# Sums of the first GNN step during the count matrix build, and GCN sums of two groups in turns

## What is computed

```python
h = jnp.maximum(_layernorm(x), 0.0)
# _L0_gnn_ref
h = jnp.tanh(h @ W_in + b_in)
for _ in range(12):
    agg = segment_sum(h[src], dst) / deg
    diff = jnp.tanh(gelu(agg @ W1 + b1) @ W2 + b2)
    h = h + (diff - decay * h) * 0.5
x = x + h
# _L1_gnn_ref, with loops added to the edges
h = jnp.maximum(_layernorm(x), 0.0)
h = relu(gcn_conv(h, W1, b1))        # gcn_conv: sum over edges of (h @ W)[src] * norm
x = x + gcn_conv(h, W2, b2)
```

## Time and profile before

| | us |
|---|---|
| median of 3 runs | 1339.37 |
| lowest, highest | 1339.19, 1340.59 |
| the profiled execution | 1339.52 |
| its span, first to last instruction | 1337.8 |
| TensorE busy in it | 1267.6 (95%) |
| VectorE busy | 400.9 (30%) |
| ScalarE busy | 314.6 (24%) |
| batches of the build | about 36 to 136 |
| twelve GNN steps | about 137 to 1181 |
| first GCN layer, second | about 1181, 1260 to the end |

### The profile page before, as it was taken

One profiled execution on the slowest core, in us unless ns is written; L12 is line 12 of the kernel. 1 busy time (PEld: TensorE's weight loads), 2 busy tenths in 40 slices (PEclk: granted clock), 3 DMA queues, 4 the chain that ended last, 5 costly groups with the idle time before them and its releaser, 6 DMA issues.

```text
span 1337.8 us, 17376 instructions
## 1 busy us (share of the span) xinstructions
PE 1267.6 (95%) x7201; PEld 712.3 (53%) x7201; DVE 400.9 (30%) x817; ACT 314.6 (24%) x449; POOL 43.5 (3%) x48
## 2 busy tenths in 40 slices
PE   2875899999999999999999999999999999979998
PEld 1764356456565564655645556456564564545545
DVE  7899113113121130121311312113122132472312
ACT  1788213113121131221311312113122131120100
POOL 4800000000000000000000000000000000000000
PEclk7899999999999999999999999999999999999999
DMA  3000200000000000000000000000000001120101
GB/s 97 1 1 0 62 0 1 0 0 0 0 0 0 0 0 0 0 0 0 0 0 0 0 0 0 0 0 0 0 0 0 0 0 40 48 59 0 49 17 33
DMA packets 24541, 13.66 MB, mean 10 GB/s; under 512 B 6171, under 2 KB 23605, under 8 KB 24384
## 3 DMA queue, kind: packets, MB, share of 16 engines
q1 hardware_dynamic: 22414, 12.28, 3.5%
q10 hardware_dynamic: 1698, 0.66, 0.2%
q0 software_dynamic: 400, 0.33, 0.1%
HBM read 9.42 MB, written 3.44 MB: 10 GB/s over the span
## 4 chain that ended last, share of the span: by engine, by line
PE 88%; DVE 7%; issue 2%; DMA 2%; ACT 0%; DVEq 0%; SPq 0%; POOL 0%; ACTq 0%; POOLq 0%
PE ps L623 66%; PE ps L670 10%; PE ps L661 9%; DVE scratch L1014 4%; PE ps L560 1%; PE ps L708 1%; DVE lo L997 1%; DMA adj<-packed_scratch,adj 1%; DMA dinv_scratch<-cols 0%; PE ps L552 0%; DMA adj<-adj 0%; PE ps L523 0%; PE ps L549 0%; DVE cols L1189 0%; DMA adj<-in_dst_dram 0%
## 5 line engine op out<-in xcount | busy, mean ns | idle before, releaser
L623 PE MATMUL ps<-adj,hi 128*128 128x512 f16 (+2 forms) x2450 | 805.8, 352 | 14.1 <-DVE lo L997 9.4
L623 PE MATMUL ps<-adj,lo 128*128 128x512 f16 (+2 forms) x2352 | 787.3, 352 | 0.0
L623 PEld LDWEIGHTS ps<-adj,hi 128*128 128x128 f16 x2450 | 237.9, 97 | 260.5 <-issue 18.8
L623 PEld LDWEIGHTS ps<-adj,lo 128*128 128x128 f16 x2352 | 228.8, 97 | 241.7 <-issue 20.6
L1120 DVE TENSOR_TENSOR ps<-ps,bias 128x512 f32<-128x512 f32 (+1 forms) x84 | 53.9, 642 | 546.5 <-PE ps L670 546.5
L825 ACT ACTIVATE scratch<-ps 128x512 f32<-128x512 f32 (+1 forms) x84 | 46.3, 551 | 630.2 <-DVE ps L1120 630.0
L670 PEld LDWEIGHTS ps<-w,scratch 128*128 128x128 f32 x1200 | 144.2, 192 | 8.1
L670 PE MATMUL ps<-w,scratch 128*128 128x128 f32 x1200 | 146.1, 275 | 0.0
L816 ACT ACTIVATE scratch<-ps,b1c,cols 128x512 f32<-128x512 f32 (+2 forms) x168 | 112.0, 723 | 144.8 <-PE ps L661 143.9
L661 PE MATMUL ps<-scratch,w 128*128 128x512 f32 (+2 forms) x336 | 137.8, 538 | 0.0
L1113 DVE TENSOR_TENSOR scratch<-ps,scratch 128x512 f32<-128x512 f32 (+2 forms) x84 | 52.0, 620 | 179.7 <-PE ps L661 132.1
(11 more groups left out here) (129 smaller groups left out, 207.2 us busy)
## 6 DMA issues: line engine op xcount, KB each, us to landing
scratch<-rdeg_scratch SPq DMA_DIRECT2D x1, 1562.5 KB
state<-in_x_dram SPq DMA_DIRECT2D x5, 256.0 KB, 4.6
scratch<-in_x_dram SPq DMA_DIRECT2D x5, 256.0 KB, 2.8
x_scratch<-state SPq DMA_DIRECT2D x5, 256.0 KB, 2.7
scratch<-dinv_scratch SPq DMA_DIRECT2D x5, 256.0 KB, 3.8
state<-x_scratch SPq DMA_DIRECT2D x5, 256.0 KB, 4.3
out_dram<-state SPq DMA_DIRECT2D x5, 256.0 KB
adj<-adj SPq DMA_DIRECT2D x1, 390.6 KB, 4.0
```

The lines of the kernel that those rows point to most:

```text
L623: return nc.tensor.matmul(bank, values[:, k, :], adj[:, k, c0:c0 + n], start=is_first, stop=is_last)
```

## The change

Three things are changed.

*Early sums.* The last 18 batches are no loop any more. Behind each batch TensorE sums two source tiles (`EARLY_TILES`) of the first step: 24 tiles of group 0 into bank 7, then 12 tiles of group 1 into bank 6, in the order `K_FIRST`, which puts the short tile last. The last window moves to bank 0. If the edge list needs the general path (`missed`, not taken with this input), they are summed again.

*The first step.* It is written out (`first_step`) on TensorE, ScalarE and VectorE. Five banks are used for the seven sums (`FIRST_BANK`); each group's tiles but the short one come first, then a wait for `s_pair`, then the short tile. `outputs` and `hidden` come one group later. Behind the last sum: `outputs(3)`, `hidden(4)`, 4 tiles of step 1, `outputs(4)`, `hidden(5)`, `hidden(6)`, 4 more tiles, `outputs(5)`, `outputs(6)`. The loop does 10 steps.

*The first GCN layer.* Behind the 4 tiles of group 0: tiles 4 to 11 of group 0, 0 to 11 of group 1, 12 to 19 of group 0, 12 to 19 of group 1 (places in `K_ORDER`), then the rest of each. VectorE makes `norm_lo(2)` earlier.

The core of the diff. Left out are helpers (`hidden`, `outputs`, `gelu`, `tanh`, `means` and others) that move out of `step` and get `t` as an argument, with `means` reading the bank of `FIRST_BANK` in the first step.

```diff
@@ -46,6 +46,8 @@
 SPANS = [(k0 * P, min(nt * P, NODES - k0 * P)) for k0, nt in GROUPS]
 K_ORDER = [(k, g) for g, (k0, nt) in enumerate(GROUPS[:TAIL]) for k in range(k0, k0 + nt) if k != SHORT]
 K_ORDER += [(SHORT, TAIL - 1), (GROUPS[TAIL][0], TAIL)]
+K_FIRST = [e for e in K_ORDER if e[0] != SHORT] + [e for e in K_ORDER if e[0] == SHORT]
+FIRST_BANK = [7, 6, 0, 1, 2, 6, 7]
 HEAD = 2 * GROUP_TILES
 LAST_HEAD = GROUP_TILES
 
@@ -66,6 +68,9 @@
 PROD_AT = [b + EVERY // 2 for b in TURN_AT]
 LO_AT = [b + 4 for b in PROD_AT]
 ENTRY_BATCHES = (LO_AT[-1] + 2) // 2 * 2
+EARLY_TILES = 2
+EARLY = EARLY_TILES * (BATCHES - ENTRY_BATCHES)
+EARLY_PARTS = [(0, min(EARLY, FULL)), (0, max(EARLY - FULL, 0))]
 PACK = 4096
 LANES = 32
 BLOCK = NODES // 5
@@ -576,11 +581,24 @@
                     entry_transpose(TURN_AT.index(b))
                 if b in PROD_AT:
                     entry_product(PROD_AT.index(b))
-            with pe.Fori(ENTRY_BATCHES // 2, BATCHES // 2) as i:
-                for u in range(2):
-                    multiply(u, i)
+            def first_sums(g, part):
+                c0, n = SPANS[g]
+                for at in range(*part):
+                    k = K_FIRST[at][0]
+                    for values in (hi, lo):
+                        if values is hi or k != SHORT:
+                            mm = nc.tensor.matmul(ps[:, FIRST_BANK[g], 0:n], values[:, k, :], adj[:, k, c0:c0 + n],
+                                                  start=(at == 0 and values is hi), stop=(k == SHORT))
+                return mm
+
+            pe.wait_ge(s_lo, NG)
+            for b in range(ENTRY_BATCHES, BATCHES):
+                multiply(b % 2, b // 2)
+                for place in range((b - ENTRY_BATCHES) * EARLY_TILES, (b - ENTRY_BATCHES + 1) * EARLY_TILES):
+                    first_sums(place // FULL, (place % FULL, place % FULL + 1))
             pe.wait_ge(s_last[0], 1)
-            window(0, 0, ps[:, 6, :], 0).then_inc(s_last[1], 1)
+            pe.wait_ge(s_ev[0], BATCHES // 2 + OPEN)
+            window(0, 0, ps[:, 0, :], 0).then_inc(s_last[1], 1)
 
             missed = pe.value_load(flag[0:1, 0:1], min_val=0, max_val=1)
 
...
                     pe.wait_ge(s_diag, 1)
                     edge_sums(STEPS, 0, (c_hi[0], c_lo[0]), 0, (0, LAST_HEAD))
                 else:
                     edge_sums(t + 1, 0, (s_hi, s_lo), (t + 1) * NG, (0, HEAD))
-                outputs(TAIL - 1)
-                outputs(TAIL)
-
-            edge_sums(0, 0, (s_hi, s_lo), 0, (0, HEAD))
-            with pe.Fori(0, STEPS - 1) as t:
+                outputs(t, TAIL - 1)
+                outputs(t, TAIL)
+
+            def first_step():
+                for g in range(NG):
+                    at = EARLY_PARTS[g][1] if g < 2 else 0
+                    if at < FULL:
+                        first_sums(g, (at, FULL))
+                    pe.wait_ge(s_pair, 16)
+                    c0, n = SPANS[g]
+                    bank = ps[:, FIRST_BANK[g], 0:n]
+                    with pe.If(missed != 0):
+                        with pe.Fori(0, TILES) as r:
+                            add_rest(0, g, bank, r)
+                    first_sums(g, (FULL, TILES)).then_inc(s_agg, 1)
+                    if g >= 3:
+                        outputs(0, g - 3)
+                    if g >= 2:
+                        hidden(0, g - 2)
+                edge_sums(1, 0, (s_hi, s_lo), NG, (0, GROUP_TILES))
+                outputs(0, TAIL - 2)
+                hidden(0, TAIL - 1)
+                hidden(0, TAIL)
+                edge_sums(1, 0, (s_hi, s_lo), NG, (GROUP_TILES, HEAD))
+                outputs(0, TAIL - 1)
+                outputs(0, TAIL)
+
+            first_step()
+            with pe.Fori(1, STEPS - 1) as t:
                 step(t, False)
             step(STEPS - 1, True)
 
@@ -710,13 +758,17 @@
                                               start=True, stop=True)
                     mm.then_inc(c_out[layer], 1)
 
+                if layer == 0:
+                    pe.wait_ge(s_diag, 2)
+                    for part in ((0, LAST_HEAD, 12), (1, 0, 12), (0, 12, 20), (1, 12, 20)):
+                        edge_sums(STEPS, part[0], (c_hi[0], c_lo[0]), 0, part[1:])
                 for g in range(NG):
                     if 2 <= g < TAIL:
                         pe.wait_ge(c_aggT[layer], g - 1)
                     if layer == 0:
                         pe.wait_ge(s_diag, g + 1)
                     edge_sums(STEPS + layer, g, (c_hi[layer], c_lo[layer]), 0,
-                              (LAST_HEAD if layer == 0 and g == 0 else 0, TILES)).then_inc(c_agg[layer], 1)
+                              (20 if layer == 0 and g < 2 else 0, TILES)).then_inc(c_agg[layer], 1)
                     if g >= 1:
                         product(g - 1)
                     if layer == 0 and g == 3:
...
-            with act.Fori(0, STEPS - 1) as t:
+                        next_hi(t, g)
+
+            act.wait_ge(s_now, 1)
+            gelu(0, 0)
+            for g in range(3):
+                tanh(0, g)
+                gelu(0, g + 1)
+            act.wait_ge(s_agg, NG)
+            next_hi(0, 0)
+            next_hi(0, 1)
+            tanh(0, 3)
+            gelu(0, 4)
+            next_hi(0, 2)
+            next_hi(0, 3)
+            tanh(0, 4)
+            gelu(0, 5)
+            gelu(0, 6)
+            next_hi(0, 4)
+            tanh(0, 5)
+            tanh(0, 6)
+            next_hi(0, 5)
+            next_hi(0, 6)
...
-                means(TAIL)
+                means(t, TAIL)
                 norm_lo(0)
-                add_bias(TAIL - 2)
+                add_bias(t, TAIL - 2)
                 norm_lo(1)
-                update(TAIL - 2)
+                update(t, TAIL - 2)
+                norm_lo(2)
                 add_input(TAIL - 2)
                 row_factors(12, 20)
                 norm_rows(3)
-                add_bias(TAIL - 1)
-                norm_lo(2)
+                add_bias(t, TAIL - 1)
                 norm_rows(4)
-                update(TAIL - 1)
+                update(t, TAIL - 1)
                 norm_lo(3)
                 add_input(TAIL - 1)
                 norm_lo(4)
-                add_bias(TAIL)
-                update(TAIL)
+                add_bias(t, TAIL)
+                update(t, TAIL)
...
-            with dve.Fori(0, STEPS - 1) as t:
+            def first_step():
+                step_scales(0)
+                means(0, 0, True)
+                means(0, 1, True)
+                for g in range(3):
+                    add_bias(0, g)
+                    update(0, g)
+                    means(0, g + 2, True)
+                dve.wait_ge(s_now, 1)
+                next_lo(0, 0)
+                add_bias(0, 3)
+                next_lo(0, 1)
+                update(0, 3)
+                means(0, 5, True)
+                means(0, 6, True)
+                add_bias(0, 4)
+                next_lo(0, 2)
+                update(0, 4)
+                next_lo(0, 3)
+                next_lo(0, 4)
+                add_bias(0, 5)
+                update(0, 5)
+                add_bias(0, 6)
+                update(0, 6)
+                next_lo(0, 5)
+                dve.wait_ge(s_hi, 2 * NG)
+                V.tensor_copy(now_keep, keep)
+                next_lo(0, 6)
+
+            first_step()
+            with dve.Fori(1, STEPS - 1) as t:
                 step(t, False)
             step(STEPS - 1, True)
```

More of the change, by code:

```diff
@@ L614, in _, with add_rest @@
                 pe.wait_ge(g_degk, 5 + OPEN)
+                for g in range(2):
+                    first_sums(g, EARLY_PARTS[g])
+            def add_rest(turn, g, bank, r):
+                n = SPANS[g][1]
+                pe.wait_ge(s_rest[g], (turn * TILES + r + 1) * 16)
+                nc.tensor.matmul(bank, hi[:, bass.ds(r, 1), :].rearrange("p k f -> p (k f)"), rest_tile[:, 0:n],
+                                 start=False, stop=False)
+                nc.tensor.matmul(bank, lo[:, bass.ds(r, 1), :].rearrange("p k f -> p (k f)"), rest_tile[:, 0:n],
+                                 start=False, stop=False).then_inc(s_restu, 1)
             def edge_sums(turn, g, split, first, part=(0, TILES)):
@@ L642, in edge_sums @@
                             with pe.Fori(0, TILES) as r:
[L643 to L647, removed]
+                                add_rest(turn, g, bank, r)
                     product(hi, k, at == 0, False)
@@ L654, in _, with hidden, outputs @@
             pe.wait_ge(s_w, 16 * 8)
-            def step(t, last):
[L656 to L673, removed]
+            def hidden(t, g):
+                n = SPANS[g][1]
+                pe.wait_ge(s_aggT, t * NG + g + 1 + OPEN)
+                pe.wait_ge(s_gelu, t * 2 * NG + (2 * g if g < TAIL else 0) + OPEN)
+                for h in range(2):
+                    nc.tensor.matmul(ps_hid_tail[h] if g == TAIL else ps_hid[h][:, 0:n], w1[:, h * FEAT:(h + 1) * FEAT],
```

(26 more changed lines are left out.)

136 lines of the change are left out of this document (69 added, 67 removed).

## The result

The changed kernel takes 1324.93 us (median of 4, 1324.38 to 1325.52) where the kernel before, run beside it, takes 1339.98: ratio 0.9889, 95% interval 0.9877 to 0.9901. The forecast was 1325.6, faster. The profiled execution has a span of 1323.0 us, 14.8 less than before.

A forecast was written before the change was run, and what follows sets the result against it. TensorE, holding 88% of the chain of waits, was taken as the bound. The start's 3.7 us (5.6 - 0.5 - 1.4) plus the GCN layer's 10.1 made 13.8: 1339.4 - 13.8 = 1325.6 us, range 1324 to 1328 (chance 0.66).

The forecast's parts named there:

- 26 at the start: Start of step 0: 72 sums done instead of 46 when the short tile's copy lands, a gain of 5.6 us.
- 40 in the layer: First GCN layer: 20 tiles of group 1 summed before the last lo rows, 8.7 us of later work done.
- The figure weighed: About 131 ns per 512-column matmul, against 216 in the trace; would give 3.4 and 5.2 us; not followed.
- the two terms: Gains from sums moved at the start of step 0 and in the first GCN layer: 5.6 and 8.7 us.
- The lag of the build: Count matrix build: delay from changes between windows and sums, put at 0.5 us, bounds 0 and 4.3.
- The slow clock behind the 14 us: Step 0, after the roughly 14 us wait for the short tile's copy: 1.4 us lost, bounds 0 and 2.7.
- The rest of step 0: Step 0 after the copy: reordered products cost nothing, tail holds by 0.6 us; about 1 us if not.
- The layer: First GCN layer: 8.7 us of work under waits plus 1.4 us for no clock fall, together 10.1 us.
- the start gives nothing: Rival on the build and step 0: only the GCN's gain is left, about 1330 us; chance 0.17.
- The low clock all through the build: Rival on the build: batches take 2.9 us at the low clock, 21 us over 18 batches, 1346.6; chance 0.04.
- the turns give half: Rival on the first GCN layer: late lo rows or a held chain; losing 5 us gives 1331; chance 0.05.
- queued behind it that don't need it: Start of step 0: 24 sums of group 1 behind the short-tile copy wait that don't need the copy; no size given.

The follow-up runs named there:

- start only: The changed kernel with its first GCN layer and VectorE's order there put back as before, keeping early sums and the new first step: 1336.49 us, ratio to before 0.9978.
- wait filled: The changed kernel with 24 sums of group 1 and 48 of group 2 ahead of the short-tile wait, first hidden product moved: 1310.24 us, ratio to before 0.9783.
- filler: The changed kernel with 56 unused matmuls between the last window and the short-tile wait: 1324.0 us, against 1325.08 for the changed kernel run beside it.
- run with 12 tiles: The changed kernel with 12 tiles of group 1 instead of 20 under the waits of the first GCN layer: 1331.01 us, ratio to before 0.9947.
- group 1 ahead: The changed kernel with only the 24 remaining sums of group 1 moved ahead of the wait for the short tile's copy: 1320.13 us, ratio to before 0.9863.
- turns only: The kernel before with only the GCN sums in turns and the earlier lo rows of group 2: 1329.41 us, ratio to before 0.9918.

## Why the prediction was right

**Pace and number.** The sums were priced by the distance of their starts and counted at the end of the wait: 26 at the start, 40 in the layer. Both counts hold. With early sums set to none the start stretch differs by two sums, with one tile a batch by none but the clock, and with 24 and 72 more sums ahead of the wait by their pace, once the clock and the copy's landing are taken off. The trace after has 0.216 between sums, as before, and the gains follow it. The figure weighed, 131 ns a matmul of 512 columns, which the Trainium skill (TensorE: Matmul & The Clock Gate, section Back-to-back issue gap) gives for a stream of loads and matmuls, would have put the two terms 5.7 us lower; the traces do not agree with it.

**The lag of the build** was put at 0.5 us and is 0 in the profile after: batches start every 1.72 us and the copy lands 15.82 us after the last. The coincidence that the forecast named, 1.72 of work in 1.72 of room, held without any cost for the change between windows and sums. But the forecast looked for the lag in that change, and where a lag shows it is the clock's. In three of the eight other profiles with early sums (start only, wait filled, filler) the first batch with sums took 2.6 to 2.7 us and not 1.71, at the low clock, and the 18 batches came 0.8 to 0.9 us late. From the start-only run:

```profile
104.50 1.66 PE L565 MATMUL ps<-scratch 128*128 128x125 f16 x12 [0.52 <-issue]
...
104.00:106.00 2.00, 1.50 (x13) 1.53 (x14) 2.00 (x3) 1.48 (x1) 0.00 (x0) 0.50 0.00 0
```

With no slack in a batch, such a fall is paid in full. That the profile after shows none is luck.

**The slow clock behind the 14 us** was put at 1.4 us and bounded by 2.7. In the profiled execution it lasted from 149.41 to about 153.4: 10 sums took 4.09 us where ten paces are 2.16, so it cost 1.9 us. In the second profile it was 14 sums, 5.88 us and 2.9 lost, past the bound. The term was mis-sized by 0.5 us in the one and 1.5 in the other, because one row of before (3.09 us for 8 sums) was taken as the size of something that varies. With the lag at 0 the two errors cancel: 5.6 - 0 - 1.9 = 3.7, as said. Measured is 3.9; of the other 0.2, 0.17 is that before the first two sums behind the wait took 0.60 us and not 0.43. So the 3.7 is right in part by luck: in the second profile of the same kernel the start gives 2.9.

**The rest of step 0** was costed at nothing. TensorE has no wait in it, and the run without early sums shows 0.41 us where two sums are 0.43. The slack of 0.6 us at its tail was enough.

**The layer** was put at 10.1 us, and is 10.04: the last lo rows did come on the old clock, the wait left is 0.33 us (0.5 said), and the clock held. The run with 12 tiles shows the two parts of it apart.

**The rivals.** That the start gives nothing is refuted by the start-only run (0.9978, interval below 1). The low clock all through the build did not come; it is at 1.00 from 100 to 120 us in the trace after, with TensorE busy for 17.64 of the 20 (the stretch is shown below), and where it came in other runs it was for one batch. That rival's price of a batch, 2.9 us, was too low besides: its 0.112 and 0.386 were read from rows in which the clock was low for a part only, while sums at the low clock start 0.43 us apart. That the turns give half was wrong; the full queue of VectorE did not matter, as the last lo rows start 17.60 us behind the last outputs' start, before 17.72.

```profile
100.00:120.00 20.00, 17.64 (x171) 12.29 (x172) 20.00 (x25) 17.12 (x13) 0.00 (x0) 1.00 0.00 1
```

What the forecast named and did not price is the largest number of the study: 24 sums "queued behind it that don't need it", and with them 48 of the next group, 14.7 us by the medians and 15.5 by the stretch.

## What to carry to other kernels

Work moved ahead of a wait is worth what TensorE has more behind it when the wait ends, not what was moved; count there, at the distance between starts. If the moved work was itself the cover of a wait, look for the next work that doesn't need what is waited for and put it in its place, since otherwise the engine stands longer and restarts at the low clock (one tile per batch: 1.58 us slower in its stretch than none). Where an accumulation waits for its last operands, a second one on another bank takes the wait's place, and filling it whole matters more than its length says, because a wait left over can bring the clock down.

## What was not expected of the hardware

**How long the clock stays low behind a wait varies.** After 5.45 us of waiting it was low for 8 sums, 3.09 us; in the start-only run, with the same code and a wait of 5.44, for 13 sums, 5.50 us. After 13.87 us it was low for 10 sums, 4.1 us, in a second profile of the same kernel for 14, 5.9 us (150.01 to 155.90). With 12 tiles in turns it was 5.5 us after a wait of only 3.79, and with group 1 ahead 5.8 us after 6.97. Such a restart cost 1.4 to 2.9 us in these traces. Nor does the length of the wait decide alone: one of 2.82 us did not bring it down, one of 3.79 did, and in the run with the turns only one of 1.82 us did (it cost nothing there, since the wait for the copy, 1.30 us long, took it up):

```profile
138.49 1.89 PE L623 MATMUL ps<-adj,hi 128*128 128x512 f16 x4 [1.82 <-ACT adj L805]
...
138.00:141.00 3.00, 2.51 (x6) 0.88 (x7) 0.56 (x3) 1.94 (x4) 0.00 (x0) 0.50 0.00 0
```

The kernel before has the same build and the same wait of 1.82 us, and there the clock stayed at 1.00:

```profile
137.36 1.04 PE L623 MATMUL ps<-adj,hi 128*128 128x512 f16 x4 [1.82 <-ACT adj L801]
...
120.00:140.00 20.00, 11.92 (x123) 8.69 (x123) 15.96 (x25) 16.53 (x13) 0.00 (x0) 1.00 0.00 1
```

What decides between the two stays open.

**Most of the spread between runs is made before the last batch.** In the twelve profiles (two of the changed kernel) the way to the first window of the last batch took 131.67 to 135.77 us. The larger part, 102.49 to 106.59, lies before batch 34, where no edit touches anything; from there to the last batch's start it takes 29.2 us in nine profiles and 30.0 to 30.1 in the three with the low clock in the first of them. From the last outputs of step 0 to those of step 11 all twelve have 950.50 or 950.51 us, and behind the first GCN product 126.8. So a microsecond of difference is read from a stretch, not from the time of a run. The granted clock has short falls to 0.50 in the run-in, at other places in each profile; that these make the spread was not tested. The nine profiles with early sums all reach batch 34 sooner (102.49 to 104.94) than the three without (105.24 to 106.59). Yet the four runs of the version with early sums set to none spread by 4.9 us by themselves, so whether the longer program has a part in it stays open too.

**A pause of about 1.1 us with no visible cause** stands nine sums behind the last window in the run with group 1 ahead, and one of 0.90 us eight matmuls behind it in the run with the filler:

```profile
139.95 10.52 PE L726 MATMUL ps<-adj,hi 128*128 128x512 f16 x48 [0.90 <-issue]
```

Both lie behind the branch over the general path. In the version with the wait filled, which has the same sums in the same place, there is none; TensorE stands there only 0.32 us at the branch. What makes it stays open.
